# Second diffusion step: ScalarE instead of VectorE scales a tile's two sums out of PSUM

## The reference

```python
for n in range(STEPS):                          # STEPS = 2
    A = _top_p_attention(Xa, W1, W2, W3)        # rows of softmax(q k^T), cut to their largest 90%
    Xf = R @ Xf                                 # R = (S + I) / row sums, S the adjacency
    Xa = A @ Xa
    Z = Z + Xf @ U1[n].T + Xa @ U2[n].T
```

## Time and profile before

| | us |
|---|---|
| median of 3 runs | 3095.23 |
| lowest and highest of them | 3094.25, 3100.11 |
| the profiled execution's own time | 3090.32 |
| span of its trace | 3088.6 |
| second diffusion step in it | about 1564 to 2368 |

### The profile page before, as it was taken

How to read it: one execution, slowest core, us unless ns; L and a number is a source line. 1 busy time by engine, 2 the same in 40 slices (tenths; PEclk the granted TensorE clock), 3 DMA queues, 4 the chain that set the end, 5 groups by cost and what they waited for, 6 DMA issues and landing times. The chain is left out here.

```text
span 3088.6 us, 44367 instructions
## 1 busy us (share of the span) xinstructions
PE 2345.9 (76%) x14134; PEld 1718.8 (56%) x14134; DVE 1944.9 (63%) x4750; ACT 1263.5 (41%) x2067; POOL 545.7 (18%) x1539
## 2 busy tenths in 40 slices
PE   3499999759455999987834975779545299999999
PEld 2377777558323877776512754657444144444458
DVE  5467667433437777776238778887883677777741
ACT  4455655231346666661256754667412200000000
POOL 0000000000014444340025543445300000000000
PEclk9699999879777999998956987889877599999999
DMA  1322122035100000000100000000003000000013
GB/s 44 115 94 94 73 90 75 5 127 196 43 16 6 23 24 19 25 23 16 44 17 5 15 11 10 11 15 16 10 10 111 40 1 0 0 0 0 0 48 93
DMA packets 49249, 120.82 MB, mean 39 GB/s; under 512 B 5904, under 2 KB 24624, under 8 KB 45744
## 3 DMA queue, kind: packets, MB, share of 16 engines
q1 hardware_dynamic: 49072, 118.83, 11.5%
HBM read 93.85 MB, written 24.97 MB: 38 GB/s over the span
## 5 line engine op out<-in xcount | busy, mean ns | idle before, releaser
L1823 DVE SCALAR_TENSOR_TENSOR fil_acc<-bank,fil_node,fil_acc 128x256 f32<-128x256 f32 x682 | 329.9, 484 | 110.3 <-PE bank L1891 97.6
L1285 PE MATMUL bank<-idf,X 128*128 128x128 f32 x968 | 137.1, 304 | 215.7 <-DVE step_recips L1750 215.7
L1362 ACT ACTIVATE step_PT<-bank 128x512 f32<-128x512 f32 (+1 forms) x264 | 128.2, 574 | 380.5 <-PE bank L1285 380.1
L1889 PE MATMUL bank<-parts_in,fil_xTh 128*128 128x512 f16 x704 | 268.3, 381 | 0.0
L1890 PE MATMUL bank<-parts_in,fil_xTh 128*128 128x512 f16 x704 | 268.0, 381 | 0.0
L1891 PE MATMUL bank<-parts_in,fil_xTl 128*128 128x512 f16 x704 | 267.8, 380 | 0.0
L1295 PE MATMUL bank<-kH,qHL 128*128 128x512 f16 (+1 forms) x264 | 104.4, 396 | 193.4 <-ACT step_E L1371 149.3
L1285 PEld LDWEIGHTS bank<-idf,X 128*128 128x128 f32 x968 | 121.5, 156 | 227.6 <-DVE step_recips L1750 219.1
L672 PE MATMUL bank<-V,HL 128*128 128x256 f32 x968 | 236.7, 386 | 0.2
L1317 PE MATMUL bank<-H,step_PT 128*128 128x256 f32 x968 | 216.0, 379 | 0.0
L1317 PE MATMUL bank<-A,step_PT 128*128 128x256 f32 x968 | 216.0, 379 | 0.0
(11 more groups left out here) (365 smaller groups left out, 5061.1 us busy)
## 6 DMA issues: line engine op xcount, KB each, us to landing
gat_A<-in_adj SPq DMA_DIRECT2D x22, 1408.0 KB, 6.0
step_a<-adjT SPq DMA_DIRECT2D x44, 352.0 KB, 3.0
gcn_raw<-in_L_W SPq DMA_DIRECT2D x16, 512.0 KB, 4.8
split<-gcn_halves SPq DMA_DIRECT2D x16, 512.0 KB, 3.4
parts_in<-split SPq DMA_DIRECT2D x4, 2048.0 KB, 19.4
adjT<-gat_a SPq DMA_DIRECT2D x22, 352.0 KB, 2.2
gcn_a<-adjT SPq DMA_DIRECT2D x22, 352.0 KB, 3.9
out_a<-adjT SPq DMA_DIRECT2D x22, 352.0 KB, 3.0
```

What stands on the lines that cost most here:

```text
L1285: last = pe.transpose(p_bank[n % nb][:, i * 128:i * 128 + 128], M[j][:, (b + i) * 128:(b + i) * 128 + 128], core.idf[:])
L1362: act.activation(PT[:, b * 128:(b + m) * 128], p_bank[n % len(p_bank)][:, 0:m * 128], ACT.Copy).then_inc(pT_done, 1)
L1823: c(dve.scalar_tensor_tensor(out=acc[k][:], in0=ps, scalar=node[k][:, n:n + 1], in1=acc[k][:], op0=ALU.mult, op1=ALU.add))
L1889: pe.matmul(w_bank[n % 4][:], xTh[k][:, x], wh[:, blk], start=c == 0, stop=False)
```

## The change

The two scalings of a tile move from VectorE's list to ScalarE's, in the second step only. They stand at the same place in the round, the head of the half. VectorE loses `take_1` and `take_0`, two instructions each. ScalarE gets `sums_1` ahead of `logits_0` and `sums_0` ahead of `logits_1`, two instructions each, that read the same columns of PSUM and write the same tiles, with the row factors handed over as a column of 128 scales in SBUF. ScalarE now waits at that place for `pv_ready`, `vt_ready` of the tile before and `p_ready`. TensorE, GpSimd and SyncE keep their lists.

```diff
+            def scaled_sums(p, q, j):
+                t = p * 2 + j
+                reuse(act, vt_ready, t, buffers=1)
+                act.wait_ge(pv_ready, t + 1)
+                act.wait_ge(p_ready, p + 1)
+                core.fence(act)
+                act.activation(va[:], pvf_bank[j][:, 0:D], ACT.Copy, scale=at(recips, q, j)).then_inc(taken, 1)
+                act.activation(vf[:], pvf_bank[j][:, D:], ACT.Copy, scale=cols(core.rdeg1, t, 1)).then_inc(taken, 1)
...
-                in_order(act, [logits_0, turned_0, products_1, exponentials_0, second_1, first_0,
-                                logits_1, turned_1, products_0, exponentials_1, second_0, first_1], T // 2)
+                sums_0, sums_1 = (2, lambda p, q: scaled_sums(p, q, 0)), (3, lambda p, q: scaled_sums(p, q, 1))
+                in_order(act, [sums_1, logits_0, turned_0, products_1, exponentials_0, second_1, first_0,
+                                sums_0, logits_1, turned_1, products_0, exponentials_1, second_0, first_1], T // 2)
...
-                in_order(dve, [take_1, largest_0, below_0, finish_1, sort_0, keep_0,
-                                take_0, largest_1, below_1, finish_0, sort_1, keep_1, check], T // 2)
+                in_order(dve, [largest_0, below_0, finish_1, sort_0, keep_0,
+                                largest_1, below_1, finish_0, sort_1, keep_1, check], T // 2)
```

## The result

| | before | after |
|---|---|---|
| median of 14 runs each | 3094.4 us | 3107.68 us |
| lowest and highest | 3090.19, 3103.63 | 3103.28, 3112.7 |
| ratio, 95% interval | | 1.0043, 1.0034 to 1.0052 |

The change makes the kernel 13.3 us slower. The profiled execution of after took 3112.7 us, the longest of its 14; that of before took 3090.32 us, close to its shortest, 3090.19. So the two traces lie further apart than the medians, and a trace's count of an event that varies between executions is not yet the kernel's.

A forecast was written before the change was run, and what follows sets the result against it. A ring of waits, turning on ScalarE's first copy in second halves, was taken as the bound. Scalings 6.8 plus clock 5.0 gave 11.8 us on the profiled 3090.3, 3102.1; with the median 4.9 above, 3107.0 us, range 3098 to 3117.

The forecast's parts named there:

- ring of waits: In the second step's rounds no engine is busy throughout; ScalarE's first copy in second halves starts the chain others wait for.
- VectorE's removal, counted 0: VectorE loses two scalings a tile, about 0.8 us earlier each half, swallowed by its later waits: 0 us.
- The pair on ScalarE, 0.38 us apart and 6.8 us in all: ScalarE's two scalings, 0.76 us ahead of the logits' copies, uncovered in nine second halves: 6.8 us (5.0 to 9.0).
- The clock, three more falls and 5.0 us: Longer TensorE waits before chunk 2 lower its clock in three more second halves, 1.67 us each: 5.0 us (0 to 10.0).
- two of three waits near 2 us: About two of three TensorE waits near 2 us cost the clock, so six of nine second halves would fall.
- Rival 1: The two scalings cost their time but TensorE's clock falls no more often: +6.8 us, 3102.0 us; chance 0.24.
- rival 2: All nine second halves lose the clock and the scalings are dear: 19 us, 3114 us; chance 0.13.
- rival 3: VectorE's list sets the pace, so ten first halves gain 0.8 us each: -8 us, 3087 us; chance 0.07.
- rival 4: No change, the scalings hide because ScalarE runs ahead of what is needed from it: 3095 us; chance 0.06.
- First halves, counted 0 within 1 us: In first halves the scalings and clock falls hide under TensorE's wait for the reciprocal: 0, within 1 us either way.

The follow-up runs named there:

- behind the copies: After with both pairs of scalings on ScalarE moved from ahead of the six copies of the logits to behind them: 3091.65 us, 1.0000 of before.
- filled kernel: After with ten TensorE matmuls that nobody reads put ahead of chunk 2 of the logits: 3102.72 us, 1.0028 of before.
- kernel with the doubled pair: After with two more scalings on ScalarE, to tiles that nobody reads, ahead of each pair: 3123.53 us, 1.0097 of before.
- only the first halves: Before with only the j = 1 scalings moved to ScalarE; VectorE keeps those of j = 0: 3088.16 us, 0.9984 of before.
- form with the stand-ins on VectorE: Only the j = 1 scalings moved to ScalarE, with two idle VectorE scalings in their old place in first halves: 3089.26 us, 0.9988 of before.
- ahead in first halves, behind in second halves: Before with both pairs moved to ScalarE, j = 1 ahead of the first half's copies, j = 0 behind the second half's: 3091.37 us, 0.9993.
- first halves and fillers: Only the j = 1 scalings moved to ScalarE, plus ten unread TensorE matmuls ahead of first-half transposes: 3091.06 us, 0.9991 of before.
- second halves alone: Before with only the j = 0 scalings moved to ScalarE; VectorE keeps those of j = 1: 3106.12 us, 1.0053 of before.
- VectorE's work put back: After with two idle scalings on VectorE where each take stood, in rounds that have logits: 3110.03 us, 1.0052 of before.
- before filled: Before with ten TensorE matmuls that nobody reads put ahead of chunk 2 of the logits: 3093.54 us, 1.0001 of before.

## Why the prediction was right

The forecast was 3107.0 us, the median is 3107.68, and the mechanism is the forecast's. That the two lie so close is luck. The sum was 11.8 us and the medians are 13.3 apart (15.9 in the later measurement); the median of before that the forecast started from was 0.8 us too high; and the sum left out terms of 4.4 us (below), while the timed medians lie some 3 us closer together than the traces.

**What bounds the kernel.** The ring of waits is confirmed by the pairs of kernels that move one thing. The pair behind the copies costs 0.0% where it costs 0.43% ahead of them, and the first halves cost nothing while the second halves carry all of it.

**VectorE's removal, counted 0.** Right for the second halves: VectorE's nine waits there grew from 27.6 to 51.2 us. For the first halves the step missed a path. The prediction let the 0.8 us go into VectorE's own next wait, for `mix` or for the logits. But ScalarE can wait for GpSimd there (0.16 us in rounds 3 and 4 of before), and GpSimd's instruction ends only behind VectorE's pass. The removal gives 0.35 us in each round whose transposes run at full clock (18.60 to 18.25 us from the reciprocal to L1404), and in kernels without the pair in the second half it spares a fall as well, 1.9 us in round 3.

**The pair on ScalarE, 0.38 us apart and 6.8 us in all.** Measured 0.35 to 0.36 us apart, 0.71 a pair, 9 x 0.71 = 6.4 us, inside 5.0 to 9.0. It lies nearer to the row from PSUM than halfway. The Trainium skill (ScalarE: Activation LUTs, What ACT_TABLE_LOAD costs) gave 0.80 us by its formula, an estimate. Its length for one column operand, an estimate of 186 + 213 + 93 = 492 ns, stands against 453 and 461 ns here; the measurement decides.

**The clock, three more falls and 5.0 us.** Of nine halves six were to fall; seven and six did, while before had three and two, so four more. A fall costs what was predicted, 1.66 us (5.46 to 7.12) against 1.67. In the traces the term is 6.3 us. The filled kernel confirms its sign in timed runs, at 4.6 and 8.7 us. The 14 runs of after agree: the granted clock averaged over a whole execution goes from 0.893 at 3104.1 us to 0.889 at 3111.2 us (correlation with the time -0.85), so much of the kernel's own scatter goes with the clock.

What length of wait costs the clock was the weakest step ("two of three waits near 2 us"). Over all 14 traces of this study (nine second and eight first halves each), how many of the waits before chunk 2 had a fall behind them:

| wait, us | second halves | first halves |
|---|---|---|
| up to 1.67 | 0 of 60 | 0 of 48 |
| 1.8 to 2.25 | 5 of 11 | - |
| 2.25 to 2.5 | 18 of 25 | 23 of 53 |
| over 2.5 | 25 of 30 | 6 of 11 |

Two thirds was about right for second halves. Rival 1 (no more falls) falls by the trace, rival 2 (all nine fall) took the kernel with the doubled pair to become true, rival 3 (VectorE sets the pace) falls by VectorE's nine waits, which grew, and rival 4 (hidden) is true only of first halves and of the place behind the copies.

**First halves, counted 0 within 1 us.** The sum is right (-0.9 us over nine rounds), the working was not complete: the relief of VectorE, which I had at nothing, makes the following wait before chunk 2 shorter, from 2.00 to 1.66 us. In "only the first halves" that spares two falls of the trace. In after it spares none, since the pair in the second half lifts that wait from 1.66 to 2.38 us again.

**What the sum left out: 3.4 us from the search to the reciprocal, and 1.0 us in the last round.** Of the 3.4 us, 1.8 are in round 9, the last but one of the nine, in a wait of VectorE's that the profile calls "remote", since it finds no instruction of this core that ended it:

```profile
2182.99 0.27 DVE L1711 SCALAR_TENSOR_TENSOR step_sel<-step_best,step_answer 128x48 f32<-128x48 f32 x1 [5.87 <-remote]
```

The one that answers to it is 4.22 and 4.21 us long in before's two traces, and 5.68 in after's second. It goes with a stall of VectorE at the head of that round (last section): the six traces that have the stall there have 5.68 to 5.87 us in this wait, the other eight 4.18 to 4.22. The rest is some 0.2 us in every round, spread over small instructions of VectorE. Nothing was run on what causes either, so this term stays open. With 6.4 + 6.3 - 0.9 + 3.4 + 1.0 the traces are 16.2 us apart; the timed medians are 13.3 apart (15.9 in the later measurement). The 3 us between these may be chance in which executions were traced, since traces of one kernel scatter by as much: they reach the first reciprocal of the table at 1677.45 and 1681.87 us before, and at 1681.20 and 1677.17 us after.

The version to keep is "only the first halves": 0.9984 of before's time (0.9975 to 0.9993), and 0.6% under after. Its form with the stand-ins on VectorE measures the same (0.9988, 0.9979 to 0.9996), so a gain clear of no change was seen twice; it is small, and at "ahead in first halves, behind in second halves" it could not be told.

## What to carry to other kernels

An engine's free time is worth something only at the place where it lies: ahead of the first copy that TensorE and VectorE both wait for, a pair of 0.71 us cost 12.7 / 9 = 1.4 us each time, the clock included, and six instructions further down the same queue it cost nothing. So before work is moved to a less busy engine, look in the timeline for its idle stretch and put the work into that, not where it stood on the other engine. And where a wait of TensorE grows, price the clock too: read from the trace after which waits it fell and kept, and follow one fall through to the next wait, since it can be hidden, move on, or even save a dearer one. A stand-in for removed work is a test only if it takes as long as what it stands for: here two instructions of 350 ns for two of 480 put back half of the time, and the half that nothing waited for.

## What the hardware showed beyond expectation

A first half and a second half of after have waits of the same 2.38 us, and in its first trace the clock fell behind none of eight in first halves, while it did behind all three such waits in second halves. In the trace taken later it fell behind three of eight. The traces don't settle whether the work ahead of the wait or chance decides. One of these waits in a first half, with the clock kept:

```profile
1779.72 0.39 PE L1295 MATMUL bank<-kH,qHL 128*128 128x512 f16 x1 [2.38 <-ACT step_E L1371]
...
1780.64 1.69 PE L1310 MATMUL bank<-F,step_a 128*128 128x256 f16 x14
```

GpSimd's small instruction L1196 (128x1) takes 0.19 us in some rounds and 2.47 in others, and what decides is VectorE. In 102 of the 126 first halves of the 14 traces it began while VectorE's pass over 2708 columns ran, and it ended 0.04 to 0.17 us behind the end of that pass, never ahead of it. In the other 24 it began after the pass and took 0.19 us. ScalarE's waits for it bear this out. So the end of a pass of VectorE sets when ScalarE gets a number that this pass has no part in.

VectorE can stand for 2 us right behind the reciprocal, at the search, with nothing to wait for that the profile shows. It happened in round 9 of after:

```profile
2127.84 0.17 DVE L1760 RECIPROCAL step_recips<-step_need 128x2 f32<-128x2 f32 x1
...
2130.05 2.98 DVE L1498 MAX8 step_top<-step_E 128x8 f32<-128x2708 f32 x1 [2.04 <-issue]
```

In both traces of after it stands in this round, and in the same one in "behind the copies", "after filled", "another pair" and "ahead and behind" (2.0 to 2.25 us). Two rounds earlier, in round 7, it stands in the kernels with first halves alone, with first halves and fillers, with second halves alone and with VectorE's work put back (0.9 to 2.1 us). No trace of before, of before filled, or of first halves with stand-ins has it. So its place goes with the program and not with chance, which speaks for how VectorE's instructions are laid out or fetched; that was not tested. Where it occurs, the search and VectorE's pass end late, ScalarE waits 0.05 to 0.20 us for GpSimd, and the chunk 2 wait (3.82 us in after) and often a fall follow from it: the round of "only the first halves" that has it lasts 67.85 us, the same round with stand-ins 64.94 us. In after, round 9 is 4.0 us longer than in before, and round 7, which is like it but has no stall, 1.2 us. So some 2.8 of the 16.2 us between the traces come with the stall and not with the pair or the clock as such, and a difference of 2 us between two of these kernels can be its place alone.
